# Filler matrix products in the opening, and three pairs of PSUM banks in the last mixture of experts

## The chip, the cores and the metric

The kernel runs on one core of a Trainium2 chip. The metric is the device time in microseconds of one execution. Engines: PE multiplies matrices (TensorE), DVE is VectorE, ACT ScalarE, POOL GpSimd, SP issues DMAs. PE's clock has two levels, 1.2 and 2.4 GHz; the profile gives the granted clock as a share of full speed.

## The reference, cut to what matters

```python
x: (8, 750, 64)                                    # batches, time, channels
h = conv1d(x, cos(phases) * w_real - sin(phases) * w_imag)     # 16 taps, 'VALID': (8, 735, 64)
n = layernorm(h)
h = h + softmax((n Wq^T) (n Wk^T)^T * 64**-0.5) n              # one head, values are n
n = layernorm(h)
logits = n @ gate_w + gate_b                       # 16 experts, the best 2 weighted by softmax
moe = sum over the 2 of  g_e * (relu(n @ w1[e] + b1[e]) @ w2[e] + b2[e])
h = h + layernorm(n + moe) * gamma + beta
```

## The kernel before, in words

The eight batches go through a software pipeline, written by hand: each engine has one instruction stream, and semaphores (`s_...`) tie the streams together. A batch has 735 positions, held as two halves of 368 columns (`HALF`) with features on partitions, or as six tiles (`NT`) of up to 128 positions with positions on partitions.

`opening()` on each engine treats batch 0 up to its gates, the convolution of batches 1 and 2 and the first maxima of batch 1. `iteration(i, ...)` then interleaves the mixture of batch i-1 with the attention of batch i (`att`), the row maxima of batch i+1 (`conv`) and the convolution of batch i+2 (`ahead`). In iteration 8 only the mixture of batch 7 is left: all blocks under `if att`, `if conv` and `if ahead` fall away.

The opening's chain for batch 0: `convolve` multiplies 8 tap pairs by two halves (16 products, 32 passes in the trace) into `small`; ACT copies it (`conv_copy`), PE transposes it (`to_tokens`), ACT copies it (`h0_copy`), DVE sums and centres it (`centre`), ACT takes the variance, POOL the reciprocal deviation (`deviation`), DVE multiplies (`normalise`), PE transposes it back (`to_features`, six transpositions), ACT and DVE split it into a rounded part and its rest (`keys_hi`, `keys_lo`), PE multiplies it by A = Wq^T Wk (`project`), ACT and DVE split that (`query_hi`, `query_lo`), and PE and DVE work out the row maxima of the six tiles in turn (`max_scores`, `reduce_max`) in the two double banks `wide[0]` and `wide[1]`. A itself is one product of the small weights that ACT rounds to `a_hi` and DVE completes with `a_lo`. The first instructions of DVE (`step`) work out the sine's argument from the phases; POOL makes the constants at the same time, the identity `ident` first.

A mixture runs over 16 experts. `first_layer(n, e)` writes the two halves of w1[e] x n into the banks `up[0]` and `up[1]`; `hide` on DVE takes bias, maximum and gate in one operation for each half and writes `hidden[:, e % 4]`; `second_layer` adds the product with w2[e] into the bank `mix`. For the experts 10, 13 and 14 (`POOLED`) ACT takes the relu (`rectify`) and POOL multiplies by the gate (`gate_hidden`; in the last iteration DVE does it). Every first layer uses the same pair of banks, so it waits for the reader of the expert before:

```python
            def first_layer(n, e, buf):
                for s in range(2):
                    if e > 0 and e - 1 in POOLED:
                        pe.wait_ge(s_relu, hidden_before(n, e - 1, s, True))
                    elif e > 0:
                        pe.wait_ge(s_hid, hidden_before(n, e - 1, s, False))
```

The gates of a batch go to DRAM in one DMA and come back in 16, one for each expert, spread over all partitions (`broadcast`, `gates_all`). After the last mixture: ACT copies `mix`, PE transposes it, DVE adds the residual (`cen2`), ACT the variance, POOL the deviation, and DVE multiplies by the deviation and by gamma and adds the rest, before the last store.

Of the kernel before, what the change touches and what calls it, by code (L numbers as in the profile page):

```python
# [90 lines left out]
def build(nc, x_t, w_real, w_imag, phases, wq, wk, gate_w, gate_b, w1, b1_t, w2, b2, gamma, beta, out):  # L91
    ctx = ExitStack()
    with ctx:
# [194 lines left out]

        def gate_hidden(eng, n, e):
# [77 lines left out]
        def _(pool):  # L367
# [8 lines left out]
                               base=0, pattern=[[-1, P]], channel_multiplier=1).then_inc(s_const, 1)  # L376
            pool.memset(power[:], -0.5).then_inc(s_const, 1)
# [82 lines left out]
        def _(act):  # L460
# [55 lines left out]
            def rectify(n, e):  # L516

                k = POOLED.index(e)
                for s in range(2):
                    act.wait_ge(s_up, 2 * E * n + 2 * e + s + 1)  # L520
                    if s == 0:
                        used = hidden_before(n, POOLED[k - 2], 1, True) if k >= 2 else hidden_before(n, e, -1, True)
                        act.wait_ge(s_phid, CREDIT + used)
                    act.activation(relu[:, k % 2, s, :], up[s][:, 0:HALF], ACT.Relu, bias=b1_pos[:, e:e + 1]).then_inc(s_relu, 1)  # L524
# [52 lines left out]
            def iteration(i, par, first, att, conv, ahead):  # L577
# [23 lines left out]
                rectify(i - 1, POOLED[0])  # L601
                if att:
                    x2_hi(i, par)
                rectify(i - 1, POOLED[1])
                if att:
                    exp_gap(i)
                rectify(i - 1, POOLED[2])
# [16 lines left out]
        def _(dve):  # L624
# [144 lines left out]
            def hide(n, e, s):  # L769
# [5 lines left out]
                dve.scalar_tensor_tensor(hidden[:, e % HIDDEN, s, :], up[s][:, 0:HALF], b1_neg[:, e:e + 1],  # L775
# [3 lines left out]
            def hide_both(n, e, att):  # L779
                if e not in POOLED:  # L780
                    hide(n, e, 0)
                    hide(n, e, 1)
# [48 lines left out]
            def opening():  # L831
# [15 lines left out]
                for t in range(NT):  # L847
# [22 lines left out]
        def _(pe):  # L870
# [5 lines left out]
            pe.wait_ge(s_const, CONST + 1)  # L876
# [46 lines left out]
            project(0)  # L923

# [90 lines left out]
            def first_layer(n, e, buf):  # L1015
                for s in range(2):
                    if e > 0 and e - 1 in POOLED:
                        pe.wait_ge(s_relu, hidden_before(n, e - 1, s, True))
                    elif e > 0:
                        pe.wait_ge(s_hid, hidden_before(n, e - 1, s, False))  # L1020
                    rhs = x2[buf][:, s * HALF:(s + 1) * HALF]
                    mm(up[s][:, 0:HALF], w1_hi[:, e, :], rhs, True, False)
                    mm(up[s][:, 0:HALF], w1_lo[:, e, :], rhs, False, True).then_inc(s_up, 1)
# [12 lines left out]

            def iteration(i, par, first, att, conv, ahead):
                m, buf = i - 1, 1 - par

                if att:  # L1040
                    pe.wait_ge(s_gtc, i)
                    transpose_max(i)
# [8 lines left out]
                if att:  # L1051
                    scores(i, 0)
                    scores(i, 1)
# [4 lines left out]
                if att:  # L1058
                    scores(i, 2)
                first_layer(m, 2, buf)  # L1060
                if att:
                    scores(i, 3)
# [3 lines left out]
                if att:  # L1066
                    pe.wait_ge(s_ftc, CREDIT + i - 1)
# [160 lines left out]
```

## Time and profile before

| | |
|---|---|
| median of 3 runs | 445.1 us (442.78 to 445.66) |
| profiled execution | 444.92 us, its span 443.0 us |
| PE busy | 392.5 us, 89% |
| DVE busy | 253.4 us, 57% |
| ACT busy | 158.0 us, 36% |
| POOL busy | 129.5 us, 29% |
| chain that ended last | PE 68%, DVE 22%, ACT 4% |

The share of an engine is an average over three stages: an opening of some 78 us, seven full iterations, and the last mixture with its end. The chain that ended last is followed back from the last instruction, so it tells in each stage whose work set the time. In rows of instructions, PE is a matrix product and PEld the load of its weights; most products are issued by one helper and have one line (L872), so they are told apart by the tile that they write.

### The profile page before, as it was taken

How to read it: one execution, taken by the hardware profiler on the slowest of the kernel's cores; microseconds unless marked ns; L12 is line 12 of the kernel's file. 1: busy time of each engine (PE TensorE's matmuls, PEld its weight loads, DVE VectorE, ACT ScalarE, POOL GpSimd, SP SyncE). 2: the span in 40 equal slices, each digit the busy share in tenths (PEclk: the TensorE clock that was granted, in tenths of full speed). 3: DMA queues.
4: the chain of work that ended last, by engine and by line, in shares of the span. 5: the costliest groups of instructions: out<-in, count | busy, mean ns of one | idle time of the engine just before them, and what ended most of it. 6: DMA issues, size and time to landing. Idle time of an engine off the chain costs nothing.

```text
span 443.0 us, 6203 instructions
## 1 busy us (share of the span) xinstructions
PE 392.5 (89%) x2188; PEld 241.4 (54%) x2188; DVE 253.4 (57%) x607; ACT 158.0 (36%) x486; POOL 129.5 (29%) x158
## 2 busy tenths in 40 slices
PE   3379778999999999999999999999999799987992
PEld 1145445666576666665666657665766565543440
DVE  3155257458745764478555855587458744654552
ACT  1234431433364335341553335432643342331021
POOL 3100120104324441245214612443244304536001
PEclk9857969999999999999999999999999999987997
DMA  7400002920086006800491029300840086008500
GB/s 188 120 0 1 1 0 95 413 80 0 7 340 241 18 2 242 344 18 2 150 413 42 0 62 399 143 1 28 330 195 18 5 295 252 19 6 337 226 0 18
DMA packets 22846, 55.91 MB, mean 126 GB/s; under 512 B 3744, under 2 KB 4768, under 8 KB 22688
## 3 DMA queue, kind: packets, MB, share of 16 engines
q1 hardware_dynamic: 22816, 55.53, 33.8%
q8 instruction: 17, 0.28, 0.3%
q14 instruction: 13, 0.11, 0.1%
HBM read 53.57 MB, written 1.95 MB: 125 GB/s over the span
## 4 chain that ended last, share of the span: by engine, by line
PE 68%; DVE 22%; ACT 4%; issue 3%; POOL 1%; SPq 1%; DMA 0%; POOLq 0%; DVEq 0%; ACTq 0%
PE up L872 18%; PE mix L872 17%; PE wide L872 13%; PE small L872 13%; DVE hidden L775 5%; DVE row_max L713 5%; PE wide L899 3%; DVE x L652 2%; ACT x L462 1%; PE wide L954 1%; DVE top_at L746 1%; PE wide L1002 1%; PE small L892 1%; DVE q_lo L652 1%; DVE attn L722 1%
## 5 line engine op out<-in xcount | busy, mean ns | idle before, releaser
L775 DVE SCALAR_TENSOR_TENSOR hidden<-up,b_neg,gates_all 128x368 f32<-128x368 f32 x208 | 115.3, 595 | 100.9 <-PE up L872 92.3
L872 PE MATMUL up<-x,w_hi 128*128 128x368 f32 x256 | 97.4, 380 | 6.5 <-DVE hidden L775 5.2
L872 PE MATMUL mix<-hidden,w2s 128*64 128x368 f32 x512 | 97.5, 499 | 0.2 <-POOL hidden L296 0.2
L872 PE MATMUL up<-x,w_lo 128*128 128x368 f32 x256 | 85.1, 332 | 0.0
L409 POOL TENSOR_SCALAR var_eps<-var 128x6 f32<-128x6 f32 x24 | 5.8, 242 | 220.6 <-ACT cen_sq L487 220.6
L872 PEld LDWEIGHTS up<-x,w_hi 128*128 128x128 f32 x256 | 48.6, 190 | 37.3 <-DVE hidden L775 18.1
L872 PEld LDWEIGHTS mix<-hidden,w2s 128*64 128x64 f32 x512 | 31.7, 139 | 39.2 <-issue 28.9
L296 POOL TENSOR_TENSOR hidden<-relu,gates_all 128x368 f32<-128x368 f32 x42 | 40.5, 986 | 40.7 <-ACT relu L524 26.4
L532 ACT ACTIVATE probs<-wide 128x736 f32<-128x736 f32 (+2 forms) x48 | 36.6, 784 | 43.4 <-PE wide L872 43.4
L872 PEld LDWEIGHTS up<-x,w_lo 128*128 128x128 f32 x256 | 49.1, 192 | 0.0
L713 DVE TENSOR_REDUCE row_max<-wide 128x1 f32<-128x736 f32 (+1 forms) x48 | 42.7, 916 | 11.1 <-PE wide L872 10.5
L487 ACT ACTIVATE cen_sq<-cen 128x64 f32<-128x64 f32 x144 | 34.6, 243 | 21.6 <-DVE cen L727 16.8
L524 ACT ACTIVATE relu<-up,b_pos 128x368 f32<-128x368 f32 x48 | 24.6, 563 | 39.1 <-PE up L872 38.6
L872 PE MATMUL wide<-q_hi,keys 128*128 128x368 f32 (+2 forms) x96 | 34.2, 356 | 0.2 <-ACT q_lo L462 0.2
L872 PE MATMUL small<-xt,conv_w 128*64 128x368 f32 x192 | 34.3, 494 | 0.0
L872 PE MATMUL small<-probs,xn 128*64 128x368 f32 (+2 forms) x192 | 33.5, 473 | 0.0
L411 POOL TENSOR_TENSOR rstd<-var_eps,power 128x6 f32<-128x6 f32 x24 | 32.4, 1351 | 2.0
L872 PE MATMUL wide<-keys,q_hi 128*128 128x368 f32 (+1 forms) x96 | 29.8, 397 | 3.5 <-DVE row_max L713 2.5
L872 PE MATMUL wide<-q_lo,keys 65*128 65x368 f32 (+2 forms) x96 | 31.9, 333 | 0.0
L487 ACT ACTIVATION_READ_ACCUMULATOR cen_sq<-cen 128x1 f32 x144 | 27.1, 188 | 0.0
L872 PEld LDWEIGHTS wide<-keys,q_hi 128*128 128x128 f32 (+1 forms) x96 | 15.4, 199 | 15.7 <-DVE row_max L713 7.3
L872 PEld LDWEIGHTS wide<-q_hi,keys 128*128 128x128 f32 (+2 forms) x96 | 17.7, 184 | 10.7 <-issue 9.1
(128 smaller groups left out, 408.3 us busy)
## 6 DMA issues: line engine op xcount, KB each, us to landing
gates_all<-gates_far SPq DMA_DIRECT2D x128, 368.0 KB, 8.2
xt<-x_t SPq DMA_DIRECT2D x8, 375.0 KB, 11.0
out<-outs SPq DMA_DIRECT2D x8, 192.0 KB, 1.8
w_raw<-w SPq DMA_DIRECT2D x2, 512.0 KB, 5.9
w2s<-w SPq DMA_DIRECT2D x1, 512.0 KB, 7.1
gates_far<-gates_t SPq DMA_DIRECT2D x8, 46.0 KB, 1.7
gates_all<-w_real SPq DMA_DIRECT2D x1, 256.0 KB, 2.6
gates_all<-w_imag SPq DMA_DIRECT2D x1, 256.0 KB, 3.1
```

What stands on the lines that cost most here:

```text
L296: eng.tensor_tensor(hidden[:, e % HIDDEN, s, :], relu[:, POOLED.index(e) % 2, s, :], gates_all[:, e, s * HALF:(s + 1) * HALF], ALU.mult).t ...
L409: pool.tensor_scalar(var_eps[k][:], var[k][:], EPS, None, ALU.add).then_inc(s_eps[k], 1)
L411: pool.tensor_tensor(rstd[k][:], var_eps[k][:], power[:], ALU.pow).then_inc(s_rstd[k], 1)
L462: return act.activation(dst, src, ACT.Copy, scale=scale)
L487: last = act.activation(cen_sq[k][:, t, :], src[:, t, :], ACT.Square, scale=D ** -0.5, accum_out=var[k][:, t:t + 1])
L524: act.activation(relu[:, k % 2, s, :], up[s][:, 0:HALF], ACT.Relu, bias=b1_pos[:, e:e + 1]).then_inc(s_relu, 1)
L532: act.activation(split(probs[0:w, t, :]), wide[t % 2][0:w, :, 0:HALF], ACT.Exp).then_inc(s_prob, 1)
L652: return dve.tensor_tensor(dst, whole, high.bitcast(F32), ALU.subtract)
L713: dve.tensor_reduce(row_max[0:w, t, D:D + 1], wide[buf][0:w, :, 0:HALF], AX.XY, ALU.max).then_inc(s_max, 1)
L775: dve.scalar_tensor_tensor(hidden[:, e % HIDDEN, s, :], up[s][:, 0:HALF], b1_neg[:, e:e + 1], gates_all[:, e, s * HALF:(s + 1) * HALF], AL ...
L872: return pe.matmul(dst, lhsT, rhs, start=start, stop=stop, skip_group_check=True)
L899: last = pe.transpose(dst[:, t % 2, j * P:j * P + w], src[0:w, t, 0:2 * D], ident[0:w, 0:w])
```

## The change

It does three things.

1. PE gets filler products in the opening (`keep_awake(n)`: n products of the identity with itself into the bank `mix`, which nobody reads at that time; 69 in all), placed after waits of their own at the steps of the chain. The first 14 stand at the start, where PE before waited for all constants; they need the identity only. The product A moves behind the first convolution. POOL's constants after the identity wait for the eighth step of the sine's argument.
2. In the last mixture (`last_mixture`, the new flag `tail`), first layers go round three pairs of banks: `up`, `wide[0]` and `wide[1]`. They wait for the reader of expert e-3, and the order on PE changes.
3. The last multiplication by gamma on DVE comes ahead of the one by the deviation.

```diff
+        def up_of(e, tail):
+            if not tail or e % 3 == 0:
+                return up[0][:, 0:HALF], up[1][:, 0:HALF]
+            return wide[e % 3 - 1][:, 0, 0:HALF], wide[e % 3 - 1][:, 1, 0:HALF]
...
+            pool.wait_ge(s_trig, 8)
             pool.memset(power[:], -0.5).then_inc(s_const, 1)
...
+            dve.wait_ge(s_cen[2], CREDIT + BATCH)
+            dve.tensor_tensor(res[0][:], cen2[:], gam[:].unsqueeze(1).broadcast_to([P, NT, D]),
+                              ALU.mult).then_inc(s_tail, 1)
+            dve.wait_ge(s_tail, 1)
             dve.wait_ge(s_rstd[2], BATCH)
-            dve.tensor_tensor(res[0][:], cen2[:], along(rstd[2][:], [P, NT, D]), ALU.mult).then_inc(s_tail, 1)
-            dve.wait_ge(s_tail, 1)
-            dve.tensor_tensor(res[1][:], res[0][:], gam[:].unsqueeze(1).broadcast_to([P, NT, D]),
-                              ALU.mult).then_inc(s_tail, 1)
+            dve.tensor_tensor(res[1][:], res[0][:], along(rstd[2][:], [P, NT, D]), ALU.mult).then_inc(s_tail, 1)
...
-            pe.wait_ge(s_const, CONST + 1)
...
+            def keep_awake(n):
+                for _ in range(n):
+                    mm(mix[:, 0:P], ident[:], ident[:], True, True)
+
+            pe.wait_ge(s_const, 2)
+            keep_awake(14)
+            pe.wait_ge(s_weff, 3)
+            convolve(0, 0, 0, CHUNKS)
             pe.wait_ge(s_wqk_in, 64)
             mm(wide[0][:, 0, 0:P], wq2[:].rearrange("o a d -> o (a d)"), wk2[:].rearrange("o a d -> o (a d)"),
                True, True).then_inc(s_a, 1)
-            pe.wait_ge(s_weff, 3)
-            convolve(0, 0, 0, CHUNKS)
+            pe.wait_ge(s_const, CONST + 1)
             pe.wait_ge(s_convc, 1)
             to_tokens(conv_t, s_ht)
+            keep_awake(2)
+            pe.wait_ge(s_h0, 1)
+            keep_awake(4)
+            pe.wait_ge(s_cen[0], 1)
+            keep_awake(6)
+            pe.wait_ge(s_var[0], 1)
+            keep_awake(6)
+            pe.wait_ge(s_rstd[0], 1)
+            keep_awake(3)
             pe.wait_ge(s_ln[0], 1)
             to_features(wide[1], xn1[0], s_t1)
+            keep_awake(3)
             pe.wait_ge(s_ahi, 1)
             pe.wait_ge(s_alo, 1)
+            pe.wait_ge(s_khi, 1)
+            keep_awake(3)
             project(0)
+            keep_awake(3)
...
-            def first_layer(n, e, buf):
+            def first_layer(n, e, buf, tail=False):
+                used = e - 3 if tail else e - 1
                 for s in range(2):
...
+            def last_mixture(n, buf):
+                first_layer(n, 0, buf, True)
+                pe.wait_ge(s_mixc, CREDIT + n)
+                pe.wait_ge(s_attn, BATCH)
+                to_tokens(moe_t, s_ft)
+                first_layer(n, 1, buf, True)
+                pe.wait_ge(s_gtc, BATCH)
+                first_layer(n, 2, buf, True)
+                gated_biases(n)
+                second_layer(n, 0)
+                for e in range(1, E - 3, 2):
+                    first_layer(n, e + 2, buf, True)
+                    first_layer(n, e + 3, buf, True)
+                    second_layer(n, e)
+                    second_layer(n, e + 1)
+                first_layer(n, E - 1, buf, True)
+                for e in range(E - 3, E):
+                    second_layer(n, e)
...
                 for t in range(NT):
                     max_scores(0, t, 1 - t % 2, t - 1)
+                    keep_awake(2)
...
+                keep_awake(1)
                 attention_to_tokens(0)
+                keep_awake(2)
+                pe.wait_ge(s_attn, 1)
+                keep_awake(4)
                 pe.wait_ge(s_h0, 2)
                 pe.wait_ge(s_ln[0], 2)
                 to_features(wide[1], xn1[1], s_t1)
+                keep_awake(3)
+                pe.wait_ge(s_khi, 2)
+                keep_awake(3)
                 project(1)
```

`hide`, `rectify` and `hide_both` take the flag too and read the banks of `up_of`. The iterations 1 to 7 keep their order on every engine.

The start of PE's stream before, with the semaphores that each instruction waits for (`small` is written by the convolution, `wide0` by the product A):

```order
L872 MATMUL wide0<-wk2,wq2 128x128 [waits wqk_loaded,constants_made]
L872 MATMUL small<-xt_0,conv_w 64x368 [waits x_loaded_0,w_eff_steps]
L872 MATMUL small<-xt_0,conv_w 64x368 x15
L892 MATMUL small<-ident,conv_t 128x128 [waits conv_copied]
L892 MATMUL small<-ident,conv_t 128x128 x2
```

The same place now (`mix<-ident` is a filler):

```order
L880 MATMUL mix<-ident 128x128 [waits constants_made]
L880 MATMUL mix<-ident 128x128 x13
L880 MATMUL small<-xt_0,conv_w 64x368 [waits x_loaded_0,w_eff_steps]
L880 MATMUL small<-xt_0,conv_w 64x368 x15
L880 MATMUL wide0<-wk2,wq2 128x128 [waits wqk_loaded]
L899 MATMUL small<-ident,conv_t 128x128 [waits conv_copied,constants_made]
L899 MATMUL small<-ident,conv_t 128x128 x2
L880 MATMUL mix<-ident 128x128 x2
L880 MATMUL mix<-ident 128x128 [waits h0_copied]
L880 MATMUL mix<-ident 128x128 x3
```

The fillers stand ahead of the convolution, the product A has moved behind it, and more fillers follow each later wait.

PE in the middle of the last mixture before, two experts (`up` is the first layer, `mix` the second):

```order
L872 MATMUL up0<-x2_1,w1_hi 128x368 [waits hidden_ready]
L872 MATMUL up0<-x2_1,w1_lo 128x368
L872 MATMUL up1<-x2_1,w1_hi 128x368 [waits hidden_ready]
L872 MATMUL up1<-x2_1,w1_lo 128x368
L872 MATMUL up0<-x2_1,w1_hi 128x368 [waits hidden_ready]
L872 MATMUL up0<-x2_1,w1_lo 128x368
L872 MATMUL up1<-x2_1,w1_hi 128x368 [waits hidden_ready]
L872 MATMUL up1<-x2_1,w1_lo 128x368
L872 MATMUL mix<-hidden,w2s 64x368 [waits hidden_ready]
```

The same place now, the first layers of two experts:

```order
L880 MATMUL wide1<-x2_1,w1_hi 128x368 [waits hidden_ready]
L880 MATMUL wide1<-x2_1,w1_lo 128x368
L880 MATMUL wide1<-x2_1,w1_hi 128x368 [waits hidden_ready]
L880 MATMUL wide1<-x2_1,w1_lo 128x368
L880 MATMUL up0<-x2_1,w1_hi 128x368 [waits hidden_ready]
L880 MATMUL up0<-x2_1,w1_lo 128x368
L880 MATMUL up1<-x2_1,w1_hi 128x368 [waits hidden_ready]
L880 MATMUL up1<-x2_1,w1_lo 128x368
L880 MATMUL mix<-hidden,w2s 64x368 [waits hidden_ready]
```

The order is the same there; the first layers write another pair each, and the wait is for a `hidden` three experts back, not one.

## Rows read from the trace of the kernel before

**Rows 1.** Busy time, granted clock and DMA by stretch, windows of core 0

```profile
18.00:34.50 16.50, 8.82 (x22) 5.16 (x22) 8.32 (x10) 5.01 (x13) 1.59 (x2) 0.50 0.00 0
55.50:61.60 6.10, 4.17 (x18) 3.50 (x18) 2.22 (x3) 2.79 (x8) 2.55 (x3) 0.50 0.00 0
62.40:399.00 336.60, 322.28 (x1886) 203.78 (x1883) 209.02 (x531) 128.39 (x393) 111.27 (x117) 0.99 0.36 137
399.30:402.00 2.70, 0.00 (x0) 0.00 (x0) 0.64 (x2) 1.57 (x10) 0.99 (x1) 1.00 0.61 171
403.50:410.50 7.00, 6.92 (x24) 3.18 (x20) 3.20 (x6) 0.00 (x0) 5.66 (x6) 0.52 1.02 409
```

**Rows 2.** Chain that ended last, opening: start us, us, what

```profile
7.58 6.93 PE small L872 x32
...
21.81 1.50 PE wide L899 x6
...
25.23 1.58 PE wide L872 x4
...
36.13 3.19 PE up L872 x12
```

**Rows 3.** Timeline, first 35 us: start us, us, engine, line, operation

```profile
1.31 0.29 POOL L375 TENSOR_SCALAR_AFFINE_SELECT ident<-ident 128x128 f32<-128x128 f32 x1
...
2.63 0.70 POOL L387 MEMSET keys<- 1x736 f32 x1
...
2.72 0.64 DVE L634 TENSOR_SCALAR trig<-trig 128x8 f32<-128x8 f32 x1
...
6.23 0.69 DVE L646 TENSOR_TENSOR conv_w<-conv_w,gates_all 128x512 f32<-128x512 f32 x1
...
7.61 0.28 ACT L462 ACTIVATE a_hi<-wide 128x128 fp32r<-128x128 f32 x1 [2.75 <-PE wide L872]
...
10.63 0.24 PEld L872 LDWEIGHTS small<-xt,conv_w 128*64 128x64 f32 x2 [0.38 <-issue]
...
11.22 0.14 PEld L872 LDWEIGHTS small<-xt,conv_w 128*64 128x64 f32 x2 [0.35 <-issue]
...
28.68 5.84 DVE L713 TENSOR_REDUCE row_max<-wide 128x1 f32<-128x736 f32 x6
```

**Rows 4.** Chain that ended last, pieces of 47 to 94 us

```profile
47.69 3.89 PE small L872 x24
...
52.13 0.95 PE small L872 x6
...
72.52 4.26 DVE row_max L713 x5
...
76.92 0.83 PE wide L954 x6
...
88.30 0.68 PE up L872 x4
...
90.45 1.39 PE mix L872 x8
...
93.70 0.87 PE up L872 x4
```

**Rows 5.** Chain that ended last, last mixture and end

```profile
401.36 0.61 DVE hidden L775
...
411.50 0.61 DVE hidden L775
...
415.23 0.61 DVE hidden L775
...
433.77 0.48 ACT moe_t L462
...
439.52 0.57 DVE res L861
```

**Rows 6.** DMA issues between 405.05 and 405.56 us (the last expert's gates)

```profile
gates_all<-gates_far SPq DMA_DIRECT2D x1, 368.0 KB, 11.1
```

More of the change, by code:

```diff
@@ L767, in gate, with hide @@
                 dve.tensor_tensor(gates[:], pick[:, 0, :, :], second, ALU.add).then_inc(s_gates, 1)
-            def hide(n, e, s):
+            def hide(n, e, s, tail):
                 dve.wait_ge(s_up, 2 * E * n + 2 * e + s + 1)
@@ L780, in hide_both @@
                 if e not in POOLED:
-                    hide(n, e, 0)
-                    hide(n, e, 1)
+                    hide(n, e, 0, not att)
+                    hide(n, e, 1, not att)
                 elif not att:
@@ L1013, in gated_biases @@
                 last.then_inc(s_bmm, 1)
-            def first_layer(n, e, buf):
+            def first_layer(n, e, buf, tail=False):
+                used = e - 3 if tail else e - 1
                 for s in range(2):
[L1017 to L1023, printed above, removed]
+                    if used >= 0 and used in POOLED:
+                        pe.wait_ge(s_relu, hidden_before(n, used, s, True))
+                    elif used >= 0:
+                        pe.wait_ge(s_hid, hidden_before(n, used, s, False))
+                    dst, rhs = up_of(e, tail)[s], x2[buf][:, s * HALF:(s + 1) * HALF]
+                    mm(dst, w1_hi[:, e, :], rhs, True, False)
+                    mm(dst, w1_lo[:, e, :], rhs, False, True).then_inc(s_up, 1)
             def second_layer(n, e):
@@ L1035, in next_max @@
                 max_scores(i + 1, t, MAX_BUF[t], MAX_FREE[t])
+            def last_mixture(n, buf):
[16 more added lines that the diff above has]
+                    second_layer(n, e)
+                pe.wait_ge(s_mixc, CREDIT + BATCH)
+                pe.wait_ge(s_ftc, CREDIT + n)
+                to_tokens(moe_t, s_ft)
             def iteration(i, par, first, att, conv, ahead):
                 m, buf = i - 1, 1 - par
-                if att:
-                    pe.wait_ge(s_gtc, i)
-                    transpose_max(i)
+                if not att:
+                    last_mixture(m, buf)
+                    return
+                pe.wait_ge(s_gtc, i)
+                transpose_max(i)
                 first_layer(m, 0, buf)
@@ L1050, in iteration @@
                     to_tokens(moe_t, s_ft)
-                if att:
-                    scores(i, 0)
-                    scores(i, 1)
+                scores(i, 0)
+                scores(i, 1)
                 first_layer(m, 1, buf)
@@ L1065, in iteration @@
                 second_layer(m, 2)
-                if att:
-                    pe.wait_ge(s_ftc, CREDIT + i - 1)
-                    weigh_values(i, 0, par)
-                if att:
-                    scores(i, 4)
+                pe.wait_ge(s_ftc, CREDIT + i - 1)
+                weigh_values(i, 0, par)
+                scores(i, 4)
                 first_layer(m, 4, buf)
-                if att:
-                    scores(i, 5)
+                scores(i, 5)
                 first_layer(m, 5, buf)
@@ L1077, in iteration @@
                 second_layer(m, 4)
-                if att:
-                    for t in range(1, 4):
-                        weigh_values(i, t, par)
+                for t in range(1, 4):
+                    weigh_values(i, t, par)
                 first_layer(m, 6, buf)
@@ L1089, in iteration @@
                 second_layer(m, 6)
[L1090 to L1092 removed]
+                weigh_values(i, 4, par)
+                weigh_values(i, 5, par)
                 if conv:
@@ L1115, in iteration @@
                 first_layer(m, 12, buf)
-                if att:
-                    pe.wait_ge(s_ln[1], i + 1)
-                    if conv:
-                        pe.wait_ge(s_max, NT * i + NT + 3)
-                    to_features(wide[1], xn2[par], s_t2)
+                pe.wait_ge(s_ln[1], i + 1)
+                if conv:
+                    pe.wait_ge(s_max, NT * i + NT + 3)
+                to_features(wide[1], xn2[par], s_t2)
                 first_layer(m, 13, buf)
```

34 lines of the change are left out of this document (11 added, 23 removed).

## The prediction

> **What bounds the kernel now.** I read first the span in stages with the granted clock, then the chain that ended last, then single rows where a term needed a price.
>
> The stages [rows 1] show three kinds of time. From 62.4 to 399 us PE is busy 322.28 of 336.60 us at a granted clock of 0.99. Nothing in the change touches the program there, so I leave that stretch as it is. Ahead of it lies an opening in which PE works 8.82 of 16.5 us at a clock of 0.50 (18.0 to 34.5) and 4.17 of 6.1 us, again at 0.50 (55.5 to 61.6). Behind it lies the last mixture, where PE stands idle from 399.3 to 402.0 and then runs at 0.52 from 403.5 to 410.5. Half clock costs time only where PE is on the chain. In the opening the chain [rows 2] is strictly serial, one engine after the other: convolution, copy, transposition, normalisation, projection, maxima. So every PE piece in it counts in full, and so does everything gained: the dense part begins earlier by what the opening loses.
>
> In the last mixture the reader is to see that the pieces of the chain alternate between PE and `hide` of DVE, and that the same piece, a `hide`, comes back after 3.73 us (411.50, 415.23) [rows 5]. In that time PE has two experts to do. With one pair of banks for the first layers, expert e+1 can't begin before `hide` of e has read them.
>
> **Part 1, the start.** Before, PE begins with the product A and the convolution starts at 7.58 [rows 2]. Its weights load in 0.24 us a pair up to 10.63 and in 0.14 from 11.22 on [rows 3]; so it runs at half clock, and rises 4.4 us after PE's first instruction at 6.8. Now 14 fills start as soon as the identity is made, at 1.60 [rows 3]. Three products of such a size take 0.95 us from first start to last end at full clock [rows 4]; in a stream one costs some 0.21, and 0.43 at half. With the same 4.4 us the clock rises at 6.0; ten fills are done then, the other four end at 6.9. The convolution's weights are ready at 6.92 (6.23 + 0.69) [rows 3], so the fills end just in time. The convolution then starts at 6.92 for 7.58, 0.66 earlier, and at full clock it takes 32/24 of 3.89 us [rows 4], 5.19, for 6.93: 1.74. Against that, A now stands behind it and ScalarE's copy of A is queued ahead of its copy of the convolution: 0.32 us for the product (a third of 0.95) and 0.28 us for the copy (`a_hi`, [rows 3]), 0.6 in all, on the path. Net **1.8 us**. If the clock rises late, the stream of fills ends at 7.6 and the convolution starts cold; that is a rival below.
>
> GpSimd's constants now wait for the eighth step of the sine's argument. DVE's small step at 2.72 took 0.64 us where its like takes 0.17 to 0.2, and it ended with GpSimd's one-row memset of `keys1` (2.63 to 3.33) [rows 3]. The wait takes that away, but weights ready 0.5 us before 6.92 are worth nothing while the fills end at 6.9. In exchange the constants run until about 7.4 beside the three weight products. Their cost lies between nothing and one more block of 0.70; I take nothing, since the blocked operation was of another kind than these products, and keep 0.7 for the range. The Trainium skill says of this on its page "SBUF — State Buffer" (section "SBUF: two separate sides") that VectorE and GpSimd share one port pair as an exclusive lock, and that a VectorE operation with two SBUF inputs is held up only by a GpSimd operation that reads SBUF. By that rule the memsets would cost the products nothing, as I take it; by the row's bound they would cost 0.7.
>
> **Part 2, first serial stretch.** Clock held at full by the fills, each PE piece takes what its like takes at full clock. Six transpositions 1.50 [rows 2] to 0.83 [rows 4]: 0.67. Projection 1.58 to 0.87, by the four passes of the same form at 93.70: 0.71. The six maxima take 5.84 us on DVE [rows 3] as PE comes late each time; five at full clock take 4.26 [rows 4], so six 5.11: 0.73, and the first starts 0.1 earlier, when DVE's `q_lo` ends. Six transpositions of the maxima, as above: 0.6. The first part of convolution 1, 3.19 [rows 2] to 12/24 of 3.89, 1.95: 1.2. Sum **4.0 us**. What hides the fills: behind `h0_copy` two and four of them (1.3 us) lie beside the copy and centring (0.5 + 1.1); six beside the variance (1.55); six and three beside GpSimd's deviation and the normalisation (1.9 + 1.0); three and three beside the two copies and `keys_lo` (0.8 + 0.95); three beside `q_hi` (0.8). In the maxima PE has 0.31 + 0.42 us of work for each 0.85 of DVE. All fit at full clock, so I cost the 69 fills at nothing. At half clock they don't fit: that is a rival.
>
> **Part 3, second serial stretch**, 53 to 62 us. Same operations: transpositions 0.6, projection 0.7, and a second set of transpositions of which 0.4 stays after the wait for `normalise` on DVE. **1.7 us**. The fills lie beside `attn`, the two normalisations, and the copies.
>
> **Part 4, last mixture.** `first_layer` of e now waits for `hide` of e-3. The first `hide` still begins at 401.36, for its gates have to land; PE has in front of it three first layers, the transposition and the biases. From there: two `hide` halves 1.11 and 0.04; second layer of 0 0.7; six steps of two first and two second layers, each 0.87 + 0.68 + 1.39 = 2.94 [rows 4] (93.70 is a first layer between work of another kind, 88.30 one that follows its like), 17.6; first layer of 15 0.87; three second layers 1.5 × 1.39 = 2.1. Sum 22.4, end 423.8. Before, the copy of the mixture begins at 433.77 [rows 5]: **9.9 us**. This takes full clock throughout. PE's idle time ahead shrinks from 2.7 us [rows 1] to some 1.4 (401.1 to 402.5), and neither of the two falls of this trace behind work came after less than 2.4 us of idle time (from the end of the 52.13 piece of [rows 4] to the second row of [rows 1], and the one here). What is late next: DVE has 1.1 per expert for PE's 1.47, so it keeps ahead. The gates land one expert about every 0.95 us; the last was issued at 405.13 and landed 11.1 us later [rows 6], at 416.2, while its `hide` is wanted at 421. So neither takes over.
>
> **Part 5, the end.** gamma is multiplied in while the deviation runs on ScalarE and GpSimd, and one DVE piece of 0.57 [rows 5] leaves the path: **0.6 us**.
>
> **Sum.** 1.8 + 4.0 + 1.7 + 9.9 + 0.6 = 18.0. The profiled execution took 444.92 us: 426.9. The median of the runs is 0.2 above it, so 427.0.
>
> **Rivals.**
> 1. The clock falls in the last mixture all the same, and comes back at 410.6 as before. For: the drop of [rows 1] came 1.2 us after PE had started again, so activity before counts, and PE still has gaps until 405. Of 7.1 us at half clock half is lost, less some 0.3 of gaps: 3.2. Time 430.2.
> 2. The clock rises late in the opening. At 402.0 PE started, and full clock came at 410.6, 8.6 us later, for 4.4 at the start. With 8.6 it rises at 10.2: the convolution starts at 7.6, has done 1.3 of 5.19 by then, and ends at 14.1 for 12.1. Time 429.0.
> 3. The fills leave a gap too many and one stretch falls to half: 4 lost, 431.
> 4. The fills run at half clock in both stretches and stand in the way. Each then costs 0.43. The 21 behind the first copy take 9.0 us where the chain needs 6.2: 2.8. Six around `keys`: 0.8. Three before the maxima: 0.5. Two in each maximum: 0.5 × 6. In the second stretch 1.1. That is 8.2, and 4.0 and 1.7 aren't gained: 440.9. Against: with its fills and pieces PE is busy some three quarters of that stretch, for 8.82 of 16.5 before [rows 1], and it enters it at full clock.
> 5. Slower than before: PE, kept at work from 1.6 us, gets half clock later on, in the dense part. Every microsecond of it costs a half, so from 36 us of half clock on the gain of 18.0 is gone; with 50 us the time is 452. Against: 0.99 over 336.6 us of much denser work [rows 1].
> 6. Half clock costs half its time wherever it is. In this kernel that would hold if PE were the chain in all of it. The three half-clock rows of [rows 1] are 29.6 us, 14.8 to be had; I count 2.8 in the first (part 2 without the convolution), 1.7 in the second and 3.2 in the third: 7.1 more, 419.8. Against: PE's busy time in the first is 8.82 of 16.5. The Trainium skill gives this as the price on its page "TensorE: Matmul & The Clock Gate" (section "Terms"): throttled time times what the ratio leaves out. By that rule 419.8, by the rows 426.9.
>
> **How the numbers follow.** Forecast 0.52, with 425 to 428.5 of its own; rival 1 0.16; rival 2 0.12; rival 3 0.07; rival 4 0.04; rival 5 0.015; rival 6 0.03; the rest to things I don't see. The range 423.5 to 431.5 holds the forecast with the 0.7 for the memsets and rivals 1 to 3, and leaves out some 0.13. A change of 1% is about what a measurement of this kernel can tell from none. Faster by over 1% (under 440.6) 0.96, within 1% 0.025 (most of rival 4), slower 0.015.
>
> **What would show it.** The convolution starts near 6.9 and ends near 12; its copy starts at 12.7. The granted clock stays 1.00 between 14 and 62 us. The first maxima take 5.1 us. The first layer of mixture 0, 77.5 before, starts near 70. Pairs of experts in the last mixture come 2.9 us apart, and PE waits there only until the third expert. One multiplication on DVE stands behind the last deviation. I am wrong if a half-clock row stands in the last mixture, if the convolution's first passes are slow, or if GpSimd's memsets stretch the weight products.

## The result, and the profile after

| | before | after |
|---|---|---|
| median | 445.38 us (4 runs, 442.78 to 447.11) | 430.13 us (4 runs, 429.19 to 431.81) |
| profiled execution | 444.92 us, span 443.0 | 430.75 us, span 428.8 |

The ratio is 0.9651, with a 95% interval of 0.9617 to 0.9686: faster by 3.5%. The time lies in the range; it is 3.1 us above the 427.0 forecast.

To see where the 14.2 us of the profiled executions came from, compare the start of the same operation in both traces: ScalarE's copy of the first convolution, 14.53 and 12.64 (1.9 gained so far); its copy of the batch's first gates, 69.36 and 65.37 (4.0); its copy of the last gates, 394.94 and 391.08 (3.9); its copy of the last mixture, 433.77 [rows 5] and 420.15 (13.6). So the opening gave 4.0, the dense part nothing (325.58 us from the first gates' copy to the last one's before, 325.71 after), the last mixture 9.8, and the end 0.5.

The stages of after, to be held against [rows 1]. The columns are the same: the window and its length, then busy us (and instructions) of PE, PEld, DVE, ACT and POOL, the granted clock, the DMA share and GB/s.

```profile
20.00:56.00 36.00, 32.30 (x205) 23.12 (x205) 19.04 (x26) 18.01 (x44) 4.15 (x5) 1.00 0.00 1
56.50:62.00 5.50, 5.47 (x22) 2.80 (x23) 3.72 (x30) 0.21 (x1) 0.00 (x0) 0.53 0.02 4
70.00:385.00 315.00, 302.77 (x1759) 192.58 (x1758) 196.98 (x465) 124.34 (x384) 107.65 (x114) 1.00 0.37 145
400.00:415.00 15.00, 15.00 (x83) 9.17 (x82) 11.96 (x24) 1.16 (x3) 4.84 (x5) 1.00 0.82 327
```

The first row is what the fillers were for: full clock where before it was 0.50. The second row is new: half clock from 56.7 to 63.7 us, where the kernel before had risen to full at 62.4. The last row shows the middle of the last mixture at full clock and without a gap.

The chain that ended last in the opening of after, against [rows 2]:

```profile
1.66 5.25 PE mix L880 x28
6.91 5.10 PE small L880 x32
12.01 0.43 PE wide L880 x2
...
19.98 0.86 PE wide L906 x6
...
22.75 0.93 PE wide L880 x4
...
25.44 5.00 DVE row_max L720 x6
...
31.39 2.00 PE up L880 x12
...
52.22 1.58 DVE xn L672
...
57.79 3.88 PE up L880 x12
61.67 2.50 PE mix L880 x26
```

The 14 fillers (28 passes) end at 6.91, and the convolution follows at full clock, 5.10 for 6.93. Transpositions, projection, maxima and convolution take 0.86, 0.93, 5.00 and 2.00 for 1.50, 1.58, 5.84 and 3.19. Then come two losses. The normalisation at 52.22 takes 1.58 where the one of the kernel before took 0.97. These are the addition on GpSimd and the normalisation, in the kernel before and then in after:

```profile
57.90 0.99 POOL L453 TENSOR_TENSOR h<-attn,h 128x384 f32<-128x384 f32 x1
58.74 0.97 DVE L665 TENSOR_TENSOR xn<-cen,rstd 128x768 f32<-128x768 f32 x1
```

```profile
51.98 1.00 POOL L460 TENSOR_TENSOR h<-attn,h 128x384 f32<-128x384 f32 x1
52.22 1.57 DVE L672 TENSOR_TENSOR xn<-cen,rstd 128x768 f32<-128x768 f32 x1
```

And from 57.79 PE works off parts of the third convolution and 26 short products, nearly all of it at half clock, 6.4 us. DVE has the gates ready at 61.93, but PE comes to their transposition only at 64.5; in the kernel before, at full clock there, PE stood ready: the gates were done at 68.49 and their transposition began at 68.53.

The last mixture of after, a piece of its chain, against [rows 5]:

```profile
394.02 4.65 DMA gates_all<-gates_far
...
398.71 0.84 PE mix L880 x4
399.55 0.88 PE up L880 x4
400.42 0.75 PE wide L880 x4
401.17 1.39 PE mix L880 x8
402.56 0.88 PE wide L880 x4
403.43 0.68 PE up L880 x4
404.11 1.39 PE mix L880 x8
405.50 1.55 PE wide L880 x8
```

No `hide` of DVE stands in it any more: from the landing of the gates on the chain is PE alone. The second layers of two experts begin at 401.17 and again at 404.11, 2.94 us apart, for 3.73 before.

### The profile page after: what moved, and what is told of

Same layout as the page of the kernel before. It is cut to its first block, busy times and chain, and to the rows that moved or that the text cites. A ratio compares the mean times of both kernels' runs of the same rounds, so it can differ in the third digit from the quotient of the medians.

```text
span 428.8 us, 6480 instructions
## 1 busy us (share of the span) xinstructions
PE 397.3 (93%) x2326; PEld 255.4 (60%) x2326; DVE 252.4 (59%) x607; ACT 157.8 (37%) x486; POOL 129.6 (30%) x158
## 3 DMA queue, kind: packets, MB, share of 16 engines
HBM read 53.57 MB, written 1.95 MB: 129 GB/s over the span
## 4 chain that ended last, share of the span: by engine, by line
PE 68%; DVE 22%; ACT 4%; issue 3%; DMA 1%; POOL 1%; POOLq 0%; SPq 0%; DVEq 0%; ACTq 0%
PE mix L880 18%; PE up L880 17%; PE wide L880 14%; PE small L880 13%; DVE row_max L720 5%; DVE hidden L782 4%; PE wide L906 3%; DVE x L659 2%; ACT x L469 1%; PE wide L1030 1%; DVE top_at L753 1%; DVE q_lo L659 1%; DVE xn L672 1%; PE wide L982 1%; PE small L899 1%
## 5 line engine op out<-in xcount | busy, mean ns | idle before, releaser
L782 DVE SCALAR_TENSOR_TENSOR hidden<-up,b_neg,gates_all 128x368 f32<-128x368 f32 x194 | 107.3, 594 | 92.8 <-PE up L880 83.6
L880 PE MATMUL mix<-hidden,w2s 128*64 128x368 f32 x512 | 94.1, 485 | 1.7 <-DVE hidden L782 1.7
L880 PE MATMUL up<-x,w_hi 128*128 128x368 f32 x236 | 87.9, 372 | 1.4 <-DVE hidden L782 0.9
L880 PE MATMUL up<-x,w_lo 128*128 128x368 f32 x236 | 77.8, 329 | 0.0
L880 PEld LDWEIGHTS up<-x,w_hi 128*128 128x128 f32 x236 | 44.3, 188 | 25.0 <-issue 13.1
L880 PEld LDWEIGHTS up<-x,w_lo 128*128 128x128 f32 x236 | 44.6, 189 | 0.0
L880 PE MATMUL small<-xt,conv_w 128*64 128x368 f32 x192 | 32.5, 472 | 0.0
L880 PE MATMUL wide<-keys,q_hi 128*128 128x368 f32 (+1 forms) x96 | 27.7, 371 | 2.7 <-DVE row_max L720 2.5
L531 ACT ACTIVATE relu<-up,b_pos 128x368 f32<-128x368 f32 x42 | 21.5, 563 | 12.1 <-PE up L880 11.5
L880 PE MATMUL mix<-ident 128*128 128x128 f32 x138 | 21.4, 300 | 3.0 <-POOL ident L381 1.7
```

Of the source, the lines that this page charges most:

```text
L531: act.activation(relu[:, k % 2, s, :], up_of(e, tail)[s], ACT.Relu, bias=b1_pos[:, e:e + 1]).then_inc(s_relu, 1)
L782: dve.scalar_tensor_tensor(hidden[:, e % HIDDEN, s, :], up_of(e, tail)[s], b1_neg[:, e:e + 1], gates_all[:, e, s * HALF:(s + 1) * HALF], A ...
L880: return pe.matmul(dst, lhsT, rhs, start=start, stop=stop, skip_group_check=True)
```

## The experiments

Each kernel starts from the changed one unless its text says otherwise. The first four were timed beside one another against the kernel before (445.5 us there), the next four likewise (445.56), the last four with more rounds (445.84). Differences of a microsecond between groups are within their intervals, so milestones of the traces carry the finer verdicts. One trace is one execution, though, and the places where the clock falls differ between executions, as the last group shows.

**tail_only.** The kernel before with `last_mixture`, `up_of` and the order of the last multiplications (PE's added waits in the opening stay, without their fillers).

> The kernel before with the last mixture in three pairs of banks and the multiplication by gamma ahead; no fillers, product A and GpSimd's constants in their old places. My theory: the two parts add up. The trace of after gives the last mixture 9.8 us (gates' first hide to the copy of the mixture) and the end 0.5 us, so 10.3 us under the kernel before, some 435. Rival: the fillers in the opening also helped the last mixture, for instance by keeping the clock up there; then this kernel shows a half-clock stretch after 400 us as the kernel before did and lies 3 us higher, near 438.

437.06 us, ratio 0.9816 (0.9791 to 0.9841). The part is worth 8.4 us by medians (445.50 - 437.06), two less than expected, and the opening's part 437.06 - 430.13 = 6.9, not the 4.0 of the first profiles. The trace decides more closely: from the copy of the last gates (396.75) to that of the mixture (425.71) it takes 28.96 us, the changed kernel 29.07, the kernel before 38.83. So the gain of the last mixture, 9.8 us, doesn't need the fillers. The rival's half clock behind 400 us isn't there. This execution had lost time elsewhere: PE began at 7.50 for 6.78 and the convolution's weights still loaded in 0.24 us a pair at 12.57 (10.63 in the kernel before), so its convolution was copied at 15.92 for 14.53. How much the start costs without fillers thus differs between executions by 1.4 us; that accounts for most of the two microseconds in this profile, and whether it does in the other three runs isn't shown.

**tail_one_pair.** The new order, one pair of banks:

```diff
-            if not tail or e % 3 == 0:
+            if True:
...
-                used = e - 3 if tail else e - 1
+                used = e - 1
```

> The changed kernel with its new order of the last mixture, but one pair of banks as before, each first layer waiting for the reader of the expert before. My theory: the gain of the last mixture is the banks' and the new order alone gives nothing or costs, since the second of two first layers now waits for a hide that itself waits for the first: pairs of experts take 3.7 us or more for 2.94, so 6 x 0.8 = 5 us over the changed kernel at the least, and up to 10 if the clock falls again. 435 to 440. Rival: the order carries the gain, then within 1 us of 430.

440.38 us (0.9842 to 0.9907), 10.2 over the changed kernel's median. Its chain, middle of the last mixture:

```profile
411.06 1.39 PE mix L880 x8
412.45 0.55 PE up L880 x2
...
413.02 0.61 DVE hidden L782
...
413.67 1.11 PE up L880 x4
414.78 1.39 PE mix L880 x8
```

The `hide` is back in the chain and two experts take 3.72 us. The mixture takes 39.18 us, before 38.83. So with one pair the new order gives nothing, and the gain needs the further banks. Three pairs in the old order were not run, so it isn't shown that the order is idle with them too. Nor is all of the 10 us the pace: six steps at 3.72 for 2.94 are 4.7. This mixture also runs at half clock from 399.8 to 406.7 and the one before from 403.7 to 410.6, the changed kernel's first profile not at all.

**tail_two_pairs.** Pairs `up` and `wide[0]`, waits for expert e-2.

```diff
-            if not tail or e % 3 == 0:
+            if not tail or e % 2 == 0:
                 return up[0][:, 0:HALF], up[1][:, 0:HALF]
-            return wide[e % 3 - 1][:, 0, 0:HALF], wide[e % 3 - 1][:, 1, 0:HALF]
+            return wide[0][:, 0, 0:HALF], wide[0][:, 1, 0:HALF]
...
-                used = e - 3 if tail else e - 1
+                used = e - 2 if tail else e - 1
```

> The changed kernel with two pairs of banks in the last mixture (up and the first wide) and waits for the reader two experts back. My theory: PE needs 2.94 us for two experts and DVE 2.1 to 2.3, so with two pairs PE waits at most a little at the first layer of e+3, which needs hide of e+1, begun only when the first layer of e+1 was done a step ahead: no wait in steady state, within 1 us of the changed kernel. Rival: the third pair is needed; a wait of some 0.5 us in each of six steps, 433.

433.01 us (0.9673 to 0.9742), 2.9 over the changed kernel's median, so more than expected. The trace splits it. Here is its chain, and behind it the window of 400 to 404 us:

```profile
399.89 2.85 PE mix L880 x8
402.74 1.52 PE wide L880 x4
404.26 1.09 PE up L880 x4
405.35 1.39 PE mix L880 x8
406.73 0.86 PE wide L880 x4
407.60 0.67 PE up L880 x4
408.26 1.39 PE mix L880 x8
```

```profile
400.00:404.00 4.00, 4.00 (x12) 1.74 (x12) 2.13 (x5) 0.00 (x0) 3.69 (x5) 0.50 1.03 415
```

In steady state the second layers come at 405.35 and 408.26, 2.91 us apart: two pairs give PE its full pace. But with two pairs PE has only two first layers to do ahead of the first `hide`, stands idle from 395.7 to 398.3, until the first half of that `hide` is done, and runs at half clock from 398.2 to 405.1. Behind that the pace is the same, so these two are the 4.1 us by which this mixture (33.18) is longer than the first profile's 29.07. Against the second profile of the changed kernel (30.56, with 3.5 us of half clock of its own) it is 2.6. My theory (no wait in steady state) was right on the pace and missed the start, the rival (a wait in each step) was wrong; the third pair is worth its work ahead of the gates.

**start_only_fills.** All lines `keep_awake(n)` but the first taken out, their waits left.

> The changed kernel without the 55 fillers behind the first convolution; the 14 at the start stay. My theory: those 55 gain 4.1 us up to 31 us of the span and 1.0 in the second serial stretch, but the half clock from 57 to 63.7 us that only the changed kernel has takes 3.1 back, so they are worth some 2.1 us net: 432.3. In the trace the granted clock falls near 16 us and near 54, and it is full again by the time of the gate logits. Rival: the half clock near 57 us has nothing to do with where the fillers stop; then it shows here too and the time is 435 or more.

433.88 us (0.9718 to 0.9767), 3.7 over the changed kernel. Two stretches:

```profile
17.00:33.00 16.00, 8.80 (x22) 5.15 (x22) 8.24 (x9) 4.54 (x9) 1.59 (x2) 0.50 0.00 0
...
54.50:60.00 5.50, 3.57 (x16) 3.12 (x14) 1.97 (x3) 2.40 (x5) 2.55 (x3) 0.50 0.00 0
61.00:66.00 5.00, 4.28 (x42) 2.61 (x39) 3.64 (x27) 0.32 (x2) 0.00 (x0) 1.00 0.02 5
```

They are the half-clock rows of the kernel before [rows 1], a little earlier, and from 61 us on the clock is full, with no fall near the gate logits. The copy of the first gates comes at 68.01, in the changed kernel's first profile at 65.37: the 55 fillers are worth 2.6 us there, as expected within 0.5. In its second profile that copy comes at 64.07 and the same fillers are worth 3.9, which is nearer to the 3.7 of the medians.

**no_first_14.** The line `keep_awake(14)` taken out.

> The changed kernel without the 14 fillers at the start; everything else stays. My theory: the convolution starts at about 6.8 as its weights are ready then, and runs at half clock for some 4.4 us, so it ends 2.0 to 2.2 us later; 432.2. Rival: the clock would have risen by itself by then, no difference.

432.37 us (0.9643 to 0.9746), 2.2 over as expected, with an interval that overlaps the changed kernel's. The convolution starts at 7.03 and takes 7.83 us; its weights load in 0.26 us a pair up to 11.96 and in 0.15 from 12.52. PE rose 5.4 us after its first work here, 4.4 us in the kernel before. The convolution's copy begins at 15.48 for 12.64, 2.8 us later, more than the 2.2 expected.

**pool_not_held.** GpSimd's wait taken out:

```diff
-            pool.wait_ge(s_trig, 8)
```

> The changed kernel without GpSimd's wait for the sine's argument, its constants stand where they stood. My theory: the sine's step is blocked for 0.5 us again by the memset of keys1, the convolution's weights come at 6.9 for 6.76, and the fillers end at 6.9 anyway: no difference that can be measured, the convolution starts at 6.8 to 7.0. Rival: the wait is what lets the convolution start in time; then 0.5 us later.

430.85 us (0.9608 to 0.9694): no difference. DVE's small step is blocked again:

```profile
2.65 0.71 DVE L640 TENSOR_SCALAR trig<-trig 128x8 f32<-128x8 f32 x1
...
6.22 0.69 DVE L652 TENSOR_TENSOR conv_w<-conv_w,gates_all 128x512 f32<-128x512 f32 x1
```

0.71 us for the 0.17 of the changed kernel; the weights are ready at 6.91 for 6.76, and the fillers end behind both (7.24 here). As the prediction had it, the wait gains nothing while the fillers end that late, and costs nothing either.

**h1_after_norm.**

```diff
                 pool.wait_ge(s_attn, 1)
+                pool.wait_ge(s_ln[1], 1)
                 pool.tensor_tensor(h1[0][:], attn[:], h0[0][:], ALU.add).then_inc(s_h1, 1)
```

> The changed kernel in which GpSimd adds h1 of batch 0 only when DVE has normalised it. My theory: in the changed kernel the normalisation of 52.22 us takes 1.57 for 0.97, because GpSimd's addition (51.98, 1.00) is under way; moved away, the normalisation takes 0.97 and the gate logits come 0.6 us earlier, 429.5. Rival: DVE's 1.57 has another cause and stays.

428.72 us (0.9576 to 0.9663), 0.8 under what was expected. DVE, then GpSimd, in this kernel:

```profile
53.16 0.96 DVE L673 TENSOR_TENSOR xn<-cen,rstd 128x768 f32<-128x768 f32 x1
```

```profile
54.27 1.00 POOL L461 TENSOR_TENSOR h<-attn,h 128x384 f32<-128x384 f32 x1 [1.32 <-DVE xn L673]
```

0.96 us for 1.57, so the addition was the cause. More instructive is what this execution did not show: its clock stays 1.00 from 50 to 70 us, without one filler more. The addition's new place can't be ruled out as a reason by this run alone, but no_first_14 and, below, end_held have the addition in its old place and no fall there either: the fall near 57 us is no fixed property of the program.

**more_fills.** Eight more fillers up to the gate logits:

```diff
                 project(1)
+                keep_awake(2)
...
                 convolve(2, 0, 0, 1, up[0])
+                keep_awake(2)
+                pe.wait_ge(s_x2hi, 1)
+                keep_awake(4)
```

> The changed kernel with 8 more fillers between the second projection and the gate logits: two behind the projection, two behind the first part of the convolution, four behind the rounding of x2. My theory: the clock stays at full from 57 to 63.7 us, PE has done its convolution and the bias products when the gates are ready, and 3.1 us come back: 427.0. Rival: the fall comes from elsewhere (the 26 short products, or the idle gap of 0.6 alone) and stays; then 430, or a little more for the fillers in the way.

429.57 us (0.9610 to 0.9654), not the 427.0 expected. Windows of it:

```profile
56.00:64.00 8.00, 7.89 (x73) 5.29 (x73) 5.29 (x33) 0.98 (x2) 0.00 (x0) 1.00 0.01 3
70.30:73.00 2.70, 2.70 (x11) 2.61 (x12) 1.46 (x3) 0.77 (x1) 0.00 (x0) 0.50 1.00 398
398.00:400.00 2.00, 2.00 (x8) 1.59 (x9) 1.00 (x3) 0.00 (x0) 1.84 (x3) 0.50 1.02 408
```

The first row and the gates' copy at 62.75 for 65.37 show 2.6 us gained. The other two show where most of it went: the clock fell at 69.7 us, behind the maxima of batch 1, and at 397.3. The mixture then took 30.48 us for 29.07. That the eight fillers gained the 2.6, or that they moved the fall on, isn't shown: end_held has none of them and its gates' copy comes at 62.75 too, and the changed kernel's second profile has both later falls beside the one near 57.

**after_again, end_held, real_work_h1, all_held.** The last four ask whether that can be covered. after_again is the changed kernel. end_held puts fillers where iteration 7 and the last mixture wait:

```diff
+                else:
+                    keep_awake(4, wide[0][:, 0, 0:P])
                 gate_logits(i, par)
...
+                if not conv:
+                    keep_awake(6, wide[0][:, 0, 0:P])
                 transpose_gates(i)
...
                 gated_biases(n)
+                pe.wait_ge(s_ftc, CREDIT + n)
+                keep_awake(6, small[:, 0:P])
                 second_layer(n, 0)
```

real_work_h1 has, beside the edit of h1_after_norm:

```diff
                 project(1)
+                keep_awake(2)
...
-                convolve(2, 0, 0, 1, up[0])
+                convolve(2, 0, 0, 3, up[0])
                 gate_logits(0, 0)
-                convolve(2, 0, 1, 4, up[0])
+                convolve(2, 0, 3, 4, up[0])
```

and all_held is both, with `keep_awake(2)` behind each of the maxima 2 to 5 of batch 1.

> The changed kernel once more, as the yardstick for the three beside it. My theory by now: its clock still falls at one or two of four places (near 57, near 70, near 386, near 398 us), which of them differs by execution, and its times scatter over 3 us for that; 430 with single runs from 428 to 432. Rival: the fall near 57 us comes in every execution, as in the first profile.

> The changed kernel with 16 more fillers near the end: four and six in iteration 7 ahead of the gate logits and of the gates' transposition (into a bank of wide), six in the last mixture ahead of the first wait for hidden (into small, after its copy). My theory: the falls near 386 and 398 us, 1.3 to 2 us each where they come, go away: 1 to 2 us under after_again, and no half clock after 380 us. Rival: PE has slack there in most runs and nothing is gained.

> The changed kernel with two further parts of the third convolution ahead of the gate logits in place of behind them, two fillers behind the second projection, and GpSimd's addition of h1 behind the normalisation. My theory: real work holds the clock as fillers do and is then not owed when the gates are ready; with the 0.6 us of the normalisation, 3 us under after_again where the clock fell near 57, 1 us where it didn't: 427.5. Rival: the convolution's parts end after x2 is ready and delay the gate logits by up to 0.5 us; no difference.

> The kernels end_held and real_work_h1 in one, with two more fillers behind each of the last four maxima of batch 1. My theory: all known places of a fall are covered; the clock is full from 6 us to the last mixture's end and the gains add: 425.5, with less scatter than the changed kernel has. Rival: fillers behind the maxima of batch 1 stand in the way of DVE's chain (PE 0.73 us for 0.85 of DVE) and cost 0.5 us each.

| | median us | six runs | ratio (interval) | mean clock of the runs |
|---|---|---|---|---|
| after_again | 431.28 | 430.09 to 432.07 | 0.9680 (0.9648 to 0.9711) | 0.980 to 0.988 |
| end_held | 429.33 | 428.92 to 430.19 | 0.9640 (0.9611 to 0.9669) | 0.989 to 0.995 |
| real_work_h1 | 428.30 | 426.91 to 431.46 | 0.9632 (0.9593 to 0.9671) | 0.987 to 0.996 |
| all_held | 428.17 | 426.98 to 428.59 | 0.9610 (0.9581 to 0.9640) | 0.994 to 0.996 |

after_again, windows at its four falls:

```profile
57.50:61.00 3.50, 3.50 (x14) 1.41 (x13) 2.87 (x27) 0.21 (x1) 0.00 (x0) 0.52 0.02 7
71.50:74.00 2.50, 2.38 (x10) 2.32 (x11) 1.26 (x3) 0.78 (x1) 0.00 (x0) 0.50 1.02 409
386.00:388.00 2.00, 2.00 (x10) 0.60 (x6) 1.90 (x21) 0.21 (x1) 0.00 (x0) 0.50 0.00 0
398.70:401.00 2.30, 2.30 (x8) 2.00 (x8) 2.30 (x6) 0.00 (x0) 2.14 (x3) 0.51 1.02 412
```

The same program that showed one fall of 7.0 us in its first profile shows four of 3.5 us each here. end_held, which has no filler between the second projection and the gate logits, at the first of these places:

```profile
58.00:60.00 2.00, 2.00 (x19) 0.92 (x16) 1.78 (x21) 0.21 (x1) 0.00 (x0) 1.00 0.05 12
```

all_held, the four places:

```profile
56.00:64.00 8.00, 6.66 (x62) 3.98 (x60) 5.10 (x33) 0.98 (x2) 0.00 (x0) 1.00 0.01 3
68.00:74.00 6.00, 5.19 (x36) 4.61 (x34) 4.11 (x8) 2.29 (x4) 0.00 (x0) 1.00 0.83 335
382.00:390.00 8.00, 7.83 (x55) 5.41 (x56) 4.95 (x33) 2.08 (x5) 3.52 (x4) 1.00 0.03 5
396.00:402.00 6.00, 5.87 (x32) 3.64 (x34) 5.41 (x12) 0.00 (x0) 5.61 (x6) 1.00 0.90 353
```

Full clock at all four, as expected; the one stretch of half clock, from 422.7 us on, comes behind PE's last product and costs nothing. The time is 3.1 us under after_again, timed beside it, with intervals that just don't overlap: faster than both kernels. Its six runs lie within 1.6 us, those of real_work_h1, where a fall is still possible near the end, within 4.6. It misses the 425.5 expected. Its gates' copy comes at 62.46, and its last mixture takes 29.44 us, the changed kernel's first profile 29.07. At the start of the last mixture the chain goes through the landing of the gates (4.65 us in the changed kernel, 4.95 in all_held, 4.48 in real_work_h1, and in end_held 7.67 for the third expert's), so clock won on PE there isn't won on the path. real_work_h1 (3.0 under after_again, as expected, the intervals overlapping) profiled at span 425.6, under all_held's 426.2, with a fall at 382 to 385.5, and its gates' copy comes at 62.60.

end_held lies 1.95 us under after_again, again with overlapping intervals, and shows no half clock from 380 us to its last product, as expected. But its profile gained elsewhere: 1.35 us from the convolution's copy to the first gates', where it has no filler more and the fall near 57 happened not to come, nothing in the dense part (325.99 for 326.02) and 0.3 in the mixture. So in this profile holding the clock at 385 and 398 us bought 0.3 us; what the other 1.6 us between the medians are isn't shown.

All profiles together split the opening behind the convolution. The time is from the start of ScalarE's copy of the first convolution to that of its copy of the first gates:

| kernels | clock | us |
|---|---|---|
| before, tail_only, start_only_fills | half in both serial stretches | 54.83, 54.94, 55.02 |
| after | half from 56.7 to 63.7 | 52.73 |
| after_again, tail_one_pair, tail_two_pairs, pool_not_held | half for 3.5 us near 57 | 51.12 to 51.15 |
| no_first_14, end_held, more_fills | full | 49.77, 49.79, 49.99 |
| h1_after_norm, real_work_h1, all_held (addition moved) | full | 49.26, 49.50, 49.49 |

A fall near 57 costs 2.9 us in the first profile and 1.3 in four others. The addition costs 0.5. Where the fall stays away, fillers or convolution parts put behind the second projection gain nothing; they stand 0.2 us in the way.

## Why the prediction held, and where it was off

- **Part 1** (1.8): 1.9 in the first profile. That is the best case on record: the copy of the first convolution begins between 12.64 and 13.59 in the eleven profiles with the 14 fillers, and the convolution starts between 6.91 and 7.86. In nine of them the fillers end last, as late as rival 2 had it (7.6) in two; in more_fills and end_held the weights are ready last, at 6.91 and 7.11. The convolution itself takes its 5.1 to 5.2 us in all of them. In the first profile the fillers end at 6.91, forecast 6.9; A and its copy cost 0.6 as summed. The 0.7 kept for memsets beside the weight products didn't occur: the product at 5.35 took 0.69 with the memset of `keys1` under way (5.34, 0.70), no more than elsewhere.
- **Part 2** (4.0): 5.93 gained when the first scores start, less 1.9: 4.0. All fillers fitted.
- **Part 3** (1.7) is the step that failed, in two ways. The clock was full there as forecast, but the normalisation, now earlier, met GpSimd's addition of h1 and took 0.6 longer, so 1.0 was left when x2 was ready (63.44 to 56.49). The collision wasn't in the sum because in the kernel before the two hardly overlapped: the normalisation started 0.84 us behind the addition of 0.99 there, and 0.24 behind it now. h1_after_norm shows cause and price. With the addition moved and no fall, the opening behind the convolution takes 49.26 to 49.50 for the 54.83 of the kernel before: 5.3 to 5.6 gained for the 5.7 of parts 2 and 3. So the prices of these two parts were right in sum, and what the sum lacked is the collision and the fall.
- **The stretch behind part 3** I left as it was, at full clock. The changed kernel fell to half there and gave back 3.0 (6.95 gained at 56.49, 3.99 at the gates' copy). So the sign "the granted clock stays 1.00 between 14 and 62 us" failed at 56.7, and the first layer of mixture 0 began at 73.5, not near 70. This is rival 3 in kind, in the next stretch, for which I had 0.07 and a price of 4. It wasn't unlikely: of the eight profiles in which the fillers stop at the second projection (after, tail_one_pair, tail_two_pairs, no_first_14, pool_not_held, h1_after_norm, after_again, end_held), five show a fall between 56 and 62 us, and the three with work put there show none. Three against eight are too few to show that this work is what holds the clock.
- **The reading behind it was wrong.** The prediction takes an idle time of 1.4 us for a safe one, since neither of "the two falls of this trace behind work" came after less than 2.4 us. The trace of the kernel before has a further fall behind work, inside the stretch that I took as a whole at 0.99:

```profile
390.40:393.80 3.40, 3.40 (x13) 1.31 (x10) 3.11 (x28) 0.21 (x1) 0.00 (x0) 0.55 0.00 0
```

  It begins at 390.0. The longest idle time of PE from 383 us up to it is 1.06 us, before the gate logits. The changed kernel has such a wait of 1.07 us before its gate logits at 56.53, and the fall comes at 56.7.
- **Part 4** (9.9): 9.8, by tail_only too. The pace was 2.94 as summed. Rival 1's fall does occur, in four of the nine profiles with three pairs and no fillers near the end (after_again, pool_not_held, h1_after_norm, more_fills), so the full clock of the first profile was in part luck. It lasts 3.5 us (3.6 in more_fills) and not 7.1; these mixtures take 30.33 to 30.56 us, the five others 28.96 to 29.93.
- **Part 5** (0.6): 0.5.

Summed, 18.0 forecast and 14.2 found in the profiled executions: 3.0 + 0.6 missing in and behind part 3. By medians it is 15.3; the runs of the kernel before lie within 4.3 us and those of the changed one within 2.6. That a good part of this is where the clock falls is likely from all_held's 1.6, but not shown. So the range held although one stretch behaved as in rival 3, because the range had been made wide enough for it, while the forecast of 427.0 itself needed a stretch without a fall. What remains open is what decides whether it falls at a given place; these traces show only that it falls at or behind places where PE has waited, and not each time.

Of the price rule of rival 6 the runs show the limit: start_only_fills is at half clock from 16.5 to 37.1 and from 54.1 to 61.0 us, 27.5 in all, and the changed kernel's first profile for 7.0. Half of the difference would be some 10 us; it is slower by 3.7 by medians, 2.7 in these two profiles.

## What to carry to other kernels

Where a serial stretch runs at half clock, fillers that fit beside the other engines' steps give back PE's share in it and nothing more. Waits that they leave behind them can still see the clock fall, in some executions and not in others, so one profile tells neither that a place is safe nor that a filler there has gained. In the last mixture, further banks of PSUM gave PE work ahead of the gates and its full pace afterwards. And when a step comes earlier, look at what it now meets: an addition on GpSimd that had been nearly over when a DVE operation began cost more than a third of that term.

## What the runs showed that I had not expected

- The clock's falls differ between executions of one program: one near 57 us in the first profile of the changed kernel, four (57.4, 71.0, 385.0, 398.7) in the second, with mean clocks from 0.980 to 0.992 over ten runs.
- An idle time of 2.6 us ahead of the gates (tail_two_pairs) was followed by half clock from 398.2 to 405.1, one of 1.7 us in the first profile of the changed kernel by none, and one of 1.2 us in its second by half clock from 398.7 to 402.2. No single length of idle time divides the cases.
- A DVE normalisation of 0.97 us took 1.57 beside GpSimd's addition when it began 0.24 us behind it, while products of DVE with two inputs took their 0.69 beside a memset of GpSimd.
